# The sine product of k on GpSimd, and two-source forms in the inverse-root chain of a recurrent and local-attention kernel

## What is computed

```python
def attn_layer(x, Wqkv, qs, ksc, Wo):
    q, k, v = jnp.split(x @ Wqkv, 3, -1)              # 16 heads of 64
    q = l2norm(q) * qs
    k = l2norm(k) * ksc
    q = q * cos * scale + rotate_half(q) * sin * scale
    k = k * cos * inv + rotate_half(k) * sin * inv
    return local_attention(q, k, v) @ Wo              # windows of 32, softmax over 64 keys
for i in range(6):
    x = attn_layer(shift_tokens(x), ...) + x
    x = ffn_layer(shift_tokens(x), ...) + x           # layer norm, W1, gelu gate, W2
```

## Time and profile before

| | |
|---|---|
| median of 3 runs | 3886.63 us (3884.57 to 3886.76) |
| the profiled execution | 3884.65 us, its span 3882.6 us |
| busy share of the span | PE 91%, DVE 81%, POOL 53%, ACT 52% |
| granted TensorE clock, mean | 0.99 |
| the 192 tile steps | from about 410 us on, some 70.8 us for each four |

### The profile page before, as it was taken

The page is one execution under the profiler, slowest core; times in us unless marked ns, Lnnn a source line. Parts: engine busy times, 40 slices in busy tenths (PEclk is TensorE's granted clock), DMA queues, the critical chain, the costliest instruction groups (busy, mean ns, idle before and its releaser), DMA issues. The chain is left out here.

```text
span 3882.6 us, 101391 instructions
## 1 busy us (share of the span) xinstructions
PE 3527.3 (91%) x42643; PEld 2214.7 (57%) x42643; DVE 3143.4 (81%) x5766; ACT 2021.7 (52%) x3871; POOL 2057.9 (53%) x1073
## 2 busy tenths in 40 slices
PE   8999689999999999999999999999999999998996
PEld 4555355555555555555555555555555555555654
DVE  3443788888888888888888888888888888888884
ACT  2222355555555555555555555555555555555553
POOL 0000465656565656556565556565565655565661
PEclk9999799999999999999999999999999999999998
DMA  2000001000001000001000001000001000000000
GB/s 64 1 1 1 7 10 31 10 7 10 10 13 32 10 10 7 10 15 31 7 10 10 7 16 31 10 7 10 10 15 29 10 10 7 13 12 15 10 10 12
DMA packets 62282, 52.53 MB, mean 14 GB/s; under 512 B 11527, under 2 KB 59397, under 8 KB 61829
## 3 DMA queue, kind: packets, MB, share of 16 engines
q1 hardware_dynamic: 61828, 46.05, 4.5%
HBM read 43.93 MB, written 2.10 MB: 12 GB/s over the span
## 5 line engine op out<-in xcount | busy, mean ns | idle before, releaser
L402 POOL TENSOR_TENSOR cosp<-cosp,rr 128x1024 f32<-128x1024 f32 x384 | 722.5, 1902 | 1095.2 <-DVE rr L65 1095.2
L412 POOL TENSOR_TENSOR cosp<-cosp,sinp 128x1024 f32<-128x1024 f32 x384 | 907.1, 2362 | 292.7 <-DVE sinp L827 292.7
L584 PEld LDWEIGHTS ps<-px,w_vo 128*128 128x128 f32 x6144 | 706.9, 192 | 201.2 <-ACT px L731 192.6
L584 PE MATMUL ps<-px,w_vo 128*128 128x128 f32 x6144 | 735.9, 278 | 56.2 <-ACT px L731 51.5
L483 PE MATMUL ps<-w_qk,xs 128*128 128x512 f32 x1536 | 749.0, 610 | 34.2 <-ACT xs L684 30.5
L695 ACT ACTIVATE sq<-ps 128x1024 f32<-128x1024 f32 x384 | 392.2, 1021 | 681.5 <-DVE sinp L827 681.5
L490 PE MATMUL ps<-ident,cosp 128*128 128x128 f32 x3072 | 417.6, 280 | 195.4 <-POOL cosp L402 182.2
L643 PE MATMUL ps<-pT,xtm 32*128 32x512 f32 x3072 | 519.7, 627 | 16.1 <-DVE w_v L892 13.0
L731 ACT COPY px<-ps 128x512 f32<-128x512 f32 x768 | 394.3, 600 | 249.0 <-PE ps L643 246.7
L490 PEld LDWEIGHTS ps<-ident,cosp 128*128 128x128 f32 x3072 | 334.6, 142 | 268.1 <-POOL cosp L402 247.4
L824 DVE TENSOR_TENSOR cosp<-ps,tab 128x1024 f32<-128x1024 f32 x384 | 462.1, 1203 | 27.4 <-PE ps L483 27.2
(11 more groups left out here) (102 smaller groups left out, 4104.7 us busy)
## 6 DMA issues: line engine op xcount, KB each, us to landing
tab<-in_tab SPq DMA_DIRECT2D x96, 128.0 KB, 2.1
qks<-in_scales SPq DMA_DIRECT2D x96, 128.0 KB, 3.2
w_qk<-in_L_ffn_Wqkv SPq DMA_DIRECT2D x12, 512.0 KB, 6.7
w_v<-in_wv_t SPq DMA_DIRECT2D x6, 512.0 KB, 8.3
w_o<-in_L_ffn_Wo SPq DMA_DIRECT2D x6, 512.0 KB, 8.9
x<-in_L_attn_x SPq DMA_DIRECT2D x16, 128.0 KB, 3.7
out<-w_v SPq DMA_DIRECT2D x16, 128.0 KB, 2.4
w<-in_L_ffn_W SPq DMA_DIRECT2D x6, 341.0 KB
```

The costliest lines, as they stand in the source:

```text
L402: eng.tensor_tensor(v, v, rr[:, B % 2, HEADS * i:HEADS * i + HEADS].unsqueeze(2).to_broadcast([P, HEADS, DH]), ALU.mult).then_inc(rot_read ...
L412: eng.tensor_tensor(cosp[:, A % 2, i, :], cosp[:, A % 2, i, :], sinp[:, i, :], ALU.add).then_inc(rot_added, 1)
L584: t = eng.matmul(S0, w_vo[:, i // HP, i % HP, :], px[:, i, :], start=i == 0, stop=i == HEADS - 1)
```

## The change

Both products of `rope` for q, and the cosine product for k, stay on DVE. The sine product for k moves: ACT copies the projected k from PSUM to a new SBUF tile `kk` (`take_k`), squares it from there, and POOL multiplies the swapped halves of `kk` by the sine table. PE's next projection now waits for that copy (`k_evac`) in place of DVE's sine product and ACT's square. In the inverse-root chain the first three operations, and the one that adds EPS to the variance (L864), get a second SBUF source each: the operand itself, or a constant tile of zeros or of the magic number. Two memsets fill these tiles at the start.

```diff
-    eng.tensor_scalar(bits, x.bitcast(I32), 1, None, ALU.logical_shift_right).then_inc(sem, 1)
-    eng.wait_ge(sem, base + 1)
-    eng.tensor_scalar(y.bitcast(I32), bits, -1, MAGIC, ALU.mult, ALU.add).then_inc(sem, 1)
+    if consts is None:
...
+    else:
+        zero, magic = consts
+        eng.scalar_tensor_tensor(out=bits, in0=x.bitcast(I32), scalar=1, in1=zero, op0=ALU.logical_shift_right, op1=ALU.bitwise_or).then_inc(sem, 1)
+        eng.wait_ge(sem, base + 1)
+        eng.scalar_tensor_tensor(out=y.bitcast(I32), in0=bits, scalar=-1, in1=magic, op0=ALU.mult, op1=ALU.add).then_inc(sem, 1)
...
# SyncE, load_table
-                    eng.wait_ge(k_roped, 2 * (ROUND * (T - 1) + 2 * w + 2))
+                    eng.wait_ge(k_cos_done, ROUND * (T - 1) + 2 * w + 2)
+                    eng.wait_ge(k_sin_done, ROUND * (T - 1) + 2 * w + 2)
# GpSimd, step
-                    for i, roped in enumerate((q_roped, k_roped)):
-                        eng.wait_ge(roped, 2 * A + 2)
-                        eng.tensor_tensor(cosp[:, A % 2, i, :], cosp[:, A % 2, i, :], sinp[:, i, :], ALU.add).then_inc(rot_added, 1)
+                    eng.wait_ge(q_roped, 2 * A + 2)
+                    eng.tensor_tensor(cosp[:, A % 2, 0, :], cosp[:, A % 2, 0, :], sinp[:, 0, :], ALU.add).then_inc(rot_added, 1)
+                    eng.wait_ge(k_evac, A + 1)
+                    after(eng, rot_added, 2 * A)
+                    sin = tab[:, A % ROUND // 2, 3, :].rearrange("p (u f) -> p u f", u=2).unsqueeze(1).to_broadcast([P, HEADS, 2, 32])
+                    eng.tensor_tensor(sinp[:, 1, :].rearrange("p (h u f) -> p h u f", u=2, f=32),
+                                      kk[:, :].rearrange("p (h u f) -> p h u f", u=2, f=32)[:, :, ::-1, :], sin, ALU.mult).then_inc(k_sin_done, 1)
+                    eng.wait_ge(k_cos_done, A + 1)
+                    eng.wait_ge(k_sin_done, A + 1)
+                    eng.tensor_tensor(cosp[:, A % 2, 1, :], cosp[:, A % 2, 1, :], sinp[:, 1, :], ALU.add).then_inc(rot_added, 1)
# TensorE, step
-                    after(eng, k_roped, 2 * A)
-                    after(eng, sq_done, 2 * A)
+                    after(eng, k_evac, A)
# ScalarE
             def square(n, i):
...
+                else:
+                    eng.wait_ge(k_evac, n + 1)
+                    eng.activation(sq[:, 1, :], kk[:, :], ACT.Square).then_inc(sq_done, 1)
+
+            def take_k(n):
+                eng.wait_ge(k_cos_done, n + 1)
+                after(eng, k_sin_done, n)
+                eng.copy(kk[:, :], R.rearrange("p a n -> p (a n)")).then_inc(k_evac, 1)
...
                 ffn(s)
                 if tile(A):
+                    take_k(A)
                     square(A, 1)
# VectorE
-                eng.tensor_scalar(ss[:, lo:hi], ss[:, lo:hi], 1e-24, None, ALU.max).then_inc(norm_step, 1)
+                eng.scalar_tensor_tensor(out=ss[:, lo:hi], in0=ss[:, lo:hi], scalar=1e-24, in1=ss[:, lo:hi], op0=ALU.max, op1=ALU.max).then_inc(norm_step, 1)
...
-                    eng.tensor_scalar(ss[:, 2 * HEADS:], aggr[:, :, 1], EPS, None, ALU.add).then_inc(stat_step, 1)
+                    eng.scalar_tensor_tensor(out=ss[:, 2 * HEADS:], in0=aggr[:, :, 1], scalar=EPS, in1=aggr[:, :, 1], op0=ALU.add, op1=ALU.max).then_inc(stat_step, 1)
```

More of the change, by code:

```diff
@@ L48, with rsqrt @@
 NT = TURNS * ROUND
-def rsqrt(eng, x, bits, half, y, sem, base):
-    eng.tensor_scalar(bits, x.bitcast(I32), 1, None, ALU.logical_shift_right).then_inc(sem, 1)
-    eng.wait_ge(sem, base + 1)
-    eng.tensor_scalar(y.bitcast(I32), bits, -1, MAGIC, ALU.mult, ALU.add).then_inc(sem, 1)
+def rsqrt(eng, x, bits, half, y, sem, base, consts=None):
+    if consts is None:
+        eng.tensor_scalar(bits, x.bitcast(I32), 1, None, ALU.logical_shift_right).then_inc(sem, 1)
+        eng.wait_ge(sem, base + 1)
+        eng.tensor_scalar(y.bitcast(I32), bits, -1, MAGIC, ALU.mult, ALU.add).then_inc(sem, 1)
+    else:
+        zero, magic = consts
+        eng.scalar_tensor_tensor(out=bits, in0=x.bitcast(I32), scalar=1, in1=zero, op0=ALU.logical_shift_right, op1=ALU.bitwise_or).then_inc(sem, 1)
+        eng.wait_ge(sem, base + 1)
+        eng.scalar_tensor_tensor(out=y.bitcast(I32), in0=bits, scalar=-1, in1=magic, op0=ALU.mult, op1=ALU.add).then_inc(sem, 1)
     n = 2
@@ L132, in build @@
         sq = sb("sq", [P, 2, INNER])
+        kk = sb("kk", [P, INNER])
         ss = sb("ss", [P, 2 * HEADS + TB])
@@ L135, in build @@
         rhalf = sb("rhalf", [P, 2 * HEADS + TB])
+        izero = sb("izero", [P, 2 * HEADS + TB], I32)
+        imagic = sb("imagic", [P, 2 * HEADS + TB], I32)
         rr = sb("rr", [P, 2, 2 * HEADS + TB])
@@ L188, in build @@
         tables_ready = sem("tables_ready")
+        consts_set = sem("consts_set")
         abc_turned = sem("abc_turned")
@@ L215, in build @@
         q_roped = sem("q_roped")
-        k_roped = sem("k_roped")
+        k_cos_done = sem("k_cos_done")
+        k_evac = sem("k_evac")
+        k_sin_done = sem("k_sin_done")
         sq_done = sem("sq_done")
@@ L692, in square @@
             def square(n, i):
-                eng.wait_ge((q_roped, k_roped)[i], 2 * n + 2)
                 after(eng, ssq_done, 2 * n - 1 + i)
-                eng.activation(sq[:, i, :], R.rearrange("p a n -> p (a n)"), ACT.Square).then_inc(sq_done, 1)
+                if i == 0:
+                    eng.wait_ge(q_roped, 2 * n + 2)
+                    eng.activation(sq[:, 0, :], R.rearrange("p a n -> p (a n)"), ACT.Square).then_inc(sq_done, 1)
+                else:
[5 more added lines that the diff above has]
+                eng.copy(kk[:, :], R.rearrange("p a n -> p (a n)")).then_inc(k_evac, 1)
             def ffn(s):
@@ L783, in _ @@
             eng.tensor_copy(mask[:, :], mask_f[:, :]).then_inc(tables_ready, 1)
+            eng.memset(izero[:, :], 0).then_inc(consts_set, 1)
+            eng.memset(imagic[:, :], MAGIC).then_inc(consts_set, 1)
+            eng.wait_ge(consts_set, 2)
             def normalise(c):
@@ L816, in rope @@
             def rope(n, i):
-                roped = (q_roped, k_roped)[i]
                 w = n % ROUND // 2
@@ L820, in rope @@
                 cos = tab[:, w, 2 * i, :].unsqueeze(1).to_broadcast([P, HEADS, DH])
-                sin = tab[:, w, 2 * i + 1, :].rearrange("p (u f) -> p u f", u=2).unsqueeze(1).to_broadcast([P, HEADS, 2, 32])
                 eng.wait_ge((q_done, k_done)[i], n + 1)
                 after(eng, turned, 4 * (n - 2) + 2 + 2 * i)
[L824 to L827, removed]
+                eng.tensor_tensor(cosp[:, n % 2, i, :].rearrange("p (h d) -> p h d", d=DH), src, cos,
+                                  ALU.mult).then_inc((q_roped, k_cos_done)[i], 1)
+                if i == 0:
+                    sin = tab[:, w, 1, :].rearrange("p (u f) -> p u f", u=2).unsqueeze(1).to_broadcast([P, HEADS, 2, 32])
+                    after(eng, rot_added, 2 * n - 1)
+                    swapped = R.rearrange("p a (h u f) -> p (a h) u f", u=2, f=32)[:, :, ::-1, :]
+                    eng.tensor_tensor(sinp[:, 0, :].rearrange("p (h u f) -> p h u f", u=2, f=32), swapped, sin, ALU.mult).then_inc(q_roped, 1)
             def square_sum(n, i):
@@ L837, in inverse_roots @@
                 base = normed(s)
-                eng.tensor_scalar(ss[:, lo:hi], ss[:, lo:hi], 1e-24, None, ALU.max).then_inc(norm_step, 1)
+                eng.scalar_tensor_tensor(out=ss[:, lo:hi], in0=ss[:, lo:hi], scalar=1e-24, in1=ss[:, lo:hi], op0=ALU.max, op1=ALU.max).then_inc(norm_step, 1)
                 eng.wait_ge(norm_step, base + 1)
-                rsqrt(eng, ss[:, lo:hi], rbits[:, lo:hi], rhalf[:, lo:hi], rr[:, s % 2, lo:hi], norm_step, base + 1)
+                rsqrt(eng, ss[:, lo:hi], rbits[:, lo:hi], rhalf[:, lo:hi], rr[:, s % 2, lo:hi], norm_step, base + 1,
+                      (izero[:, lo:hi], imagic[:, lo:hi]))
             def glu(T, m, k):
```

## The result

The changed kernel takes 4087.7 us (median; 4086.0 to 4087.89) against 3886.4 us before: ratio 1.0521, 95% interval 1.0508 to 1.0534. It is slower by 201 us. The prediction said slower, 4035 us, range 3860 to 4150. So the direction and the range were right, and the size was short by 53 us.

The account below looks back on a forecast made before the run. The prediction took the end of DVE's inverse-root chain, through L402 to PE's k-turn, as the bound. Its step terms summed to 3.1 us a turn, x 48 = 149 us, on 3886.63: 4035 us, range 3860 to 4150.

Parts of the forecast that it names:

- S3: One of a turn's four steps: chain due 2.15 us earlier but waiting for GpSimd's addition and table product; -0.7 us.
- S0: One of a turn's four steps: chain due at 2041.2 stands until GpSimd's k-addition ends at 2043.5; +2.1 us.
- S1: One of a turn's four steps: GpSimd is done before the chain starts, 0.5 us to spare; 0 us.
- S2: One of a turn's four steps: ACT's gelu ends late, the chain waits 1.8 us for GpSimd's k-addition; +1.7 us.
- What bounds the kernel: In every step PE's k-turn waits 0.69 to 0.77 us for L402, which waits for DVE's inverse-root chain.
- The two-source forms wait: DVE chain operations with two SBUF sources wait for GpSimd like one-source ones; forecast case 3960 to 4075 us, chance 0.66.
- the list of signs: Expected in the changed profile: chain's first operation over 1.5 us in S0 and S2, about 1 in S3, 0.2 in S1.
- the third rival: GpSimd holds the path for part of its instruction only, so the chain threads between: 3840 to 3960 us; chance 0.08.
- The sine product: k's sine product added to GpSimd behind ACT's copy: taken as 2.36 us, bounds 1.88 and 2.91.
- the second rival: GpSimd's sine product is dear, over 2.6 us: 4075 to 4210 us when the chain waits; chance 0.08.
- The sum of the waits: Changes of the four steps, -0.7 + 2.1 + 0 + 1.7 = 3.1 us a turn, x 48 = 149 us.
- The first rival: Two-source chain operations in S0, S2 and S3 do not wait for GpSimd: -91 us, 3795 us; chance 0.18.

Follow-up runs that it names:

- clock kept up: Changed kernel plus four idle-time products on PE ahead of the q-turn in both the S0-to-S1 and S3-to-S0 steps: 4017.6 us, ratio 1.0342.
- the PSUM chain: Changed kernel with the inverse-root chain's intermediate numbers in PSUM, at most one SBUF source per operation: 3782.4 us, ratio 0.9739.

## Why the prediction was right, and where it was short

| step | before | forecast | after | after, clock kept up |
|---|---|---|---|---|
| S3 | 19.34 | 18.6 | 18.41 | 18.42 |
| S0 | 16.14 | 18.2 | 18.87 | 17.99 |
| S1 | 17.90 | 17.9 | 18.67 | 17.93 |
| S2 | 17.46 | 19.2 | 19.17 | 19.18 |
| turn | 70.84 | 73.9 | 75.12 | 73.52 |

*What bounds the kernel.* The chain's end, through L402, to the k-turn: right in every step of after, where GpSimd's wait ends with the chain all 192 times. With the sine product on VectorE, one operation fewer in the chain takes 42 us off (3827.9 to 3786.0), some 0.22 a step; with it on GpSimd and the chain free, three steps of four follow the chain.

*The two-source forms wait.* Right: 1.88, 0.93 and 0.65, and 2.33 us in S2, S3 and S0. In S0 it is the chain's second operation that waits, as the first (0.19) slips in ahead of the addition, which the sum allowed for and the list of signs did not. Each held operation ends 0.05 us behind GpSimd's instruction, so the third rival (held for a part only) falls. The two reasons given, that a second SBUF stream comes at no cost in time and that a one-source cast runs at twice the rate, pointed to a shared second path; the PSUM chain fits it, as operations with at most one SBUF source and the rest in PSUM run free. That it is a path, and not some other property of these forms, the runs do not show by themselves: of the one-source operations from SBUF to SBUF, `tensor_scalar` is held, and the reciprocal and the aggregation are not.

*The sine product.* Taken as 2.36; the mean of its 192 instances is 2.37, so the second rival (over 2.6) falls. ScalarE's copy was taken as 1.02 and takes 1.01.

*The sum of the waits.* Forecast 3.1 us a turn, 149 us; measured with the clock kept up 73.52 - 70.84 = 2.7 a turn, 131 us. Each step is within 0.25 us of its forecast. The terms that were too large: in S3 the chain was due when forecast, but GpSimd's addition, which it waits for, ended 0.14 us earlier and the table product behind it 0.15. In S0 the addition ended 0.1 us earlier, and the chain was due 0.33 earlier, since its start did follow from the product taken off VectorE, against the forecast; so its first operation slipped in.

*The term that was missing.* The clock. I worked the sum at the clock of before and asked, of each wait, only how late it makes the next thing. The waits also leave PE standing 1.11, 1.55 and 0.77 us one after another in S0's step, and behind that PE ran 3.4 us at half speed, on the path: 70 us in all. The trace of before had the warning: PE there idled at most 0.77 us in these places and its clock stayed at 1.00, but in the last layer, where it stood 2.60 us for `w_v`, the clock was 0.50 for 3.4 us from 3516.9 on. The 53 us by which the forecast fell short are these 70, less the 18 by which the waits were oversized.

*The first rival* (two-source operations do not wait, 3795 us) describes a kernel that was then built by other means: with the chain free of GpSimd it measured 3782.4 us, and S3 17.25 us against the 17.2 that the rival's terms give.

## What to carry to other kernels

When work moves to GpSimd, look at what VectorE will be doing while it runs there. Here `scalar_tensor_tensor` with two SBUF sources, and `tensor_scalar` from SBUF to SBUF, were held to the end of GpSimd's instruction at 4 to 36 numbers a partition, while the same forms with at most one SBUF source and the rest in PSUM ran on, and so did a reciprocal and `bn_aggr` from SBUF to SBUF. A `tensor_tensor` with two SBUF sources was not seen under a GpSimd instruction. Such a wait shows as a long instruction, not as idle time, so compare a line's shortest and median duration. And where a change makes PE stand longer, add what the clock may take on top of the wait.

## What the runs showed of the hardware that was not expected

The fall of the clock moves: filled idle time in one step sent it to another step's idle 1.69 us in part of the turns, and filling both kept the granted clock at 1.00 (the second place alone was not tried). In the changed kernel that second place stands idle 1.68 us as well and no fall follows, so the length of one idle piece does not tell by itself. And operations of 128x32 numbers cost the same with PSUM operands as in SBUF, 0.19 to 0.20 us, so a chain in PSUM is not slower than one in SBUF. Of one-source operations from SBUF to SBUF some are held by GpSimd (`tensor_scalar`, L864 at 1359 ns in the median) and some are not (the aggregation just before it, 148 ns).
